# Attention with paired heads: all 64 rows of each half of the array filled in the score matmuls

## The reference

```
mod = (silu(c) @ wmod).reshape(8, 6, 1, 256)      # sa, ca, ga, sb, cb, gb; |gates| at least 0.25
h = layernorm(x) * (1 + ca) + sa
q, k, v = split(h @ w_in.T)                       # 16 heads of 16 columns
attn = softmax(causal(q @ k.T * 16 ** -0.5))      # 1024 x 1024 for each head
x = x + ga * ((attn @ v) @ w_out.T + b_out)
h = layernorm(x) * (1 + cb) + sb
r = sigmoid(mix(h, mu_r) @ W_r); kk = relu(mix(h, mu_k) @ W_k) ** 2
out = x + gb * (r * (kk @ W_v))                   # mix: a blend of each token with the one before it
```

## Time and the profile before

| what | value |
|---|---|
| time, median of 3 runs | 1929.98 us (1923.19 to 1935.57) |
| the profiled execution | 1931.11 us, span 1929.2 us |
| mean granted clock of TensorE | 0.798 |
| TensorE busy | 1640.5 us (85%) |
| VectorE busy | 1100.7 us (57%) |
| ScalarE busy | 924.7 us (48%) |
| GpSimd busy | 618.7 us (32%) |

### The profile page before, as it was taken

One profiled execution on the slowest core, in us unless ns is written; L12 is line 12 of the kernel. 1 busy time (PEld: TensorE's weight loads), 2 busy tenths in 40 slices (PEclk: granted clock), 3 DMA queues, 4 the chain that ended last, 5 costly groups with the idle time before them and its releaser, 6 DMA issues.

```text
span 1929.2 us, 34555 instructions
## 1 busy us (share of the span) xinstructions
PE 1640.5 (85%) x10856; PEld 929.0 (48%) x10856; DVE 1100.7 (57%) x2246; ACT 924.7 (48%) x1859; POOL 618.7 (32%) x750
## 2 busy tenths in 40 slices
PE   4698999898889989889898988889888998988854
PEld 2353445444554545454554545445454454544354
DVE  4656646756565655756566564666656555666232
ACT  2055545555455544545554553554544455545512
POOL 3012102433333332443323333333324432233455
PEclk7696859788986888778896787968897688978656
DMA  2311122111321122111221112211231112111100
GB/s 93 81 38 40 44 82 57 39 46 47 92 55 37 48 56 82 40 48 48 85 57 34 44 47 85 58 40 38 63 87 40 48 45 68 49 46 37 51 29 17
DMA packets 79864, 103.37 MB, mean 54 GB/s; under 512 B 22576, under 2 KB 43320, under 8 KB 79680
## 3 DMA queue, kind: packets, MB, share of 16 engines
q1 hardware_dynamic: 76544, 91.86, 17.4%
q0 software_dynamic: 2560, 8.39, 1.2%
q10 hardware_dynamic: 576, 0.79, 0.2%
HBM read 31.74 MB, written 8.94 MB: 21 GB/s over the span
## 4 chain that ended last, share of the span: by engine, by line
PE 63%; DVE 19%; issue 8%; ACT 5%; POOL 2%; SPq 1%; DMA 1%; DVEq 0%; ACTq 0%; POOLq 0%
PE val_ps L1120 14%; PE row_ps L1088 11%; PE col_ps L1051 10%; DVE max_a L874 9%; PE dense_ps L1130 8%; PE dense_ps L1132 6%; PE dense_ps L1131 6%; PE row_ps L1099 4%; PE dense_ps L1149 2%; DVE mixed L982 2%; DVE max_b L874 2%; ACT weights L715 1%; DVE gated L966 1%; DVE mix_out L990 1%; PE row_ps L1069 1%
## 5 line engine op out<-in xcount | busy, mean ns | idle before, releaser
L715 ACT ACTIVATE weights<-col_ps 128x512 f32<-128x512 f32 (+2 forms) x1280 | 635.3, 557 | 644.1 <-PE col_ps L1051 639.0
L874 DVE TENSOR_REDUCE max_a<-row_ps 128x1 f32<-128x512 f32 (+3 forms) x896 | 541.8, 644 | 402.2 <-PE row_ps L1099 251.4
L1088 PE MATMUL row_ps<-k_stack,q_stack 48*128 48x512 f32 (+3 forms) x1536 | 467.7, 469 | 108.8 <-DVE max_a L874 77.4
L1051 PE MATMUL col_ps<-q_stack,k_stack 50*128 50x512 f32 (+3 forms) x1536 | 425.8, 466 | 45.9 <-ACT weights L715 37.2
L604 POOL TENSOR_SCALAR_AFFINE_SELECT weights<-weights 128x512 f32<-128x512 f32 x256 | 169.0, 660 | 845.7 <-ACT weights L715 844.3
L1120 PE MATMUL val_ps<-weights,v_ones 128*32 128x512 f32 (+3 forms) x3072 | 405.0, 606 | 3.9 <-POOL weights L604 3.9
L1088 PEld LDWEIGHTS row_ps<-k_stack,q_stack 48*128 48x128 f32 x1536 | 228.0, 223 | 340.1 <-DVE max_a L874 186.4
L874 DVE TENSOR_REDUCE max_b<-row_ps 128x1 f32<-128x384 f32 (+3 forms) x384 | 215.1, 594 | 199.3 <-PE row_ps L1099 197.0
L1051 PEld LDWEIGHTS col_ps<-q_stack,k_stack 50*128 50x128 f32 x1536 | 212.8, 219 | 135.6 <-ACT weights L715 82.7
L1099 PE MATMUL row_ps<-mask_fill,mask_ident 64*128 64x64 bf16 (+1 forms) x2048 | 165.7, 233 | 0.0
L1120 PEld LDWEIGHTS val_ps<-weights,v_ones 128*32 128x32 f32 x3072 | 65.6, 118 | 88.8 <-issue 41.7
(11 more groups left out here) (122 smaller groups left out, 2173.3 us busy)
## 6 DMA issues: line engine op xcount, KB each, us to landing
q_stack<-q_part SPq DMA_DIRECT2D x384, 64.0 KB, 2.2
k_stack<-k_part SPq DMA_DIRECT2D x372, 64.0 KB, 2.2
xa<-in_x SPq DMA_DIRECT2D x8, 1024.0 KB, 5.6
att<-val_out SPq DMA_DIRECT2D x64, 128.0 KB
recips<-recip_rows SPq DMA_DIRECT2D x32, 256.0 KB
xq<-in_x SPq DMA_DIRECT2D x28, 256.0 KB, 3.7
out<-xq POOLq DMA_DIRECT2D x28, 256.0 KB, 2.8
q_stack<-max_rows SPq DMA_DIRECT2D x256, 4.0 KB
```

Source lines behind the costliest of these rows:

```text
L715: nc.scalar.activation(weights[:, t % 2, heads[0]:heads[-1] + 1:2, 0:q1 - q0], col_ps[bank][:, 0:n * (q1 - q0)].rearrange("p (h q) -> p h ...
L874: nc.vector.reduce_max(dest, bank[:, 0:len(heads) * (k1 - k0)].rearrange("p (h k) -> p h k", h=len(heads)), AX_X).then_inc(max_done, 1)
L1051: last = nc.tensor.matmul(col_ps[bank][:, i * (q1 - q0):(i + 1) * (q1 - q0)], stack_at(k_stack[s % 2], rows, heads[i], P * j, P * (j + 1)) ...
L1088: last = nc.tensor.matmul(banks[odd][:, n * width:(n + 1) * width], stack_at(q_stack[stack], rows, heads[n], P * i, P * (i + 1)), stack_at ...
```

## The change

The maximum's two rows move from rows 48 and 49 of each half to rows 62 and 63. The 14 rows between, 48 to 61, are now in the contraction: they are zero in `q_stack`, set once at the start by GpSimd, and 1.0 in `k_stack`, as they were before, so that they add nothing to a score. `row_pair` contracts 62 rows for each head in place of 48, `score_columns` 64 in place of 50.

```
--- before.py
+++ after.py
@@ -44,6 +44,7 @@
 ROWS = len(Q_PARTS) * HD
 MROWS = 2
 ROW_TILE = 64
+MAX_AT = ROW_TILE - MROWS
 FILL = 2 * 2 * len(Q_PARTS) * 16
 PLACED = 2 * MROWS * 16
 
@@ -463,7 +464,7 @@
 
                 for part in range(MROWS):
                     for odd in range(2):
-                        row, lo = ROW_TILE * odd + ROWS + part, 8 * (2 * part + odd)
+                        row, lo = ROW_TILE * odd + MAX_AT + part, 8 * (2 * part + odd)
                         sp.dma_start(stack[row:row + 1, half].rearrange("p g n -> p (g n)").bitcast(F32),
                                      max_rows[half][lo:lo + 8, :].bitcast(F32)).then_inc(max_placed[half], 16)
 
@@ -569,8 +570,10 @@
             nc.gpsimd.memset(ident[:], 0.0)
             nc.gpsimd.memset(mask_ident[:], 0.0)
             nc.gpsimd.memset(mask_fill[:], 0.0)
-            nc.gpsimd.memset(neg_half[:], -0.5).then_inc(consts_zero, 1)
-            pool.wait_ge(consts_zero, 1)
+            nc.gpsimd.memset(neg_half[:], -0.5)
+            for stack in q_stack:
+                nc.gpsimd.memset(stack[:].bitcast(F32), 0.0).then_inc(consts_zero, 1)
+            pool.wait_ge(consts_zero, 2)
             nc.gpsimd.affine_select(out=ident[:], in_=ident[:], compare_op=ALU.not_equal, fill=1.0, base=0,
                                     pattern=[[-1, P]], channel_multiplier=1).then_inc(consts_done, 1)
 
@@ -1047,7 +1050,7 @@
                         bank, ago = bank_of(COLS * s + c + odd, COLS * G)
                         if i == 0:
                             wait(pe, exp_done, exp_index(b, s, c + odd) + (1 - ago))
-                        rows = slice(ROW_TILE * odd, ROW_TILE * odd + ROWS + MROWS)
+                        rows = slice(ROW_TILE * odd, ROW_TILE * (odd + 1))
                         last = nc.tensor.matmul(col_ps[bank][:, i * (q1 - q0):(i + 1) * (q1 - q0)],
                                                 stack_at(k_stack[s % 2], rows, heads[i], P * j, P * (j + 1)),
                                                 stack_at(q_stack[s % 2], rows, heads[i], q0, q1),
@@ -1083,7 +1086,7 @@
                     for odd, heads in enumerate(pair):
                         if n == 0:
                             banks[odd] = row_bank(b, s, u + odd)
-                        rows = slice(ROW_TILE * odd, ROW_TILE * odd + ROWS)
+                        rows = slice(ROW_TILE * odd, ROW_TILE * odd + MAX_AT)
                         end = n == len(heads) - 1 and not diagonal
                         last = nc.tensor.matmul(banks[odd][:, n * width:(n + 1) * width],
                                                 stack_at(q_stack[stack], rows, heads[n], P * i, P * (i + 1)),
```

## The result

The changed kernel takes 1844.28 us (median of 4 runs, 1840.81 to 1848.19), against 1926.59 us for the kernel before on the same chip: a ratio of 0.9571, 95% interval 0.9523 to 0.9619, so 4.3% faster. The forecast was 2.3% (1886 us): the sign, and the clock as the way to it, were as forecast; the size was almost twice that. The profiled execution takes 1840.81 us, its span 1838.9, at a mean granted clock of 0.865 against 0.798.

A forecast was written before the change was run, and what follows sets the result against it. TensorE was taken as the bound, busy 85% at a mean clock of 0.798. All costs were 0; the clock gain of 44 us took 1931.1 to 1887, 1886 us at the median, range 1860 to 1912.

The forecast's parts named there:

- Three steps were taken at zero: Costs of more rows in score matmuls and weight loads, of the maximum's moved DMAs, and of two GpSimd memsets: each 0.
- the bound of zero: Weight loads of the score matmuls: extra rows cost between zero and 19 us in all; zero was taken.
- a cover that reached to 19 us: At the start, TensorE's first products end at 19.0 us, before it needs the constants, which the memsets delay to about 7.5.
- the forecast's case against the rule of the Trainium skill: Score stretches 5.00 of 5.00 us busy had clock 0.50, so busy share doesn't set it; the rule would leave 1930 us.
- The rival in which zero data doesn't count: Part of the no-change rival: the clock grant ignores rows whose data is zero; 1930 us, chance 0.32 for no change.
- Three of twelve are 15 us in a batch: Of twelve low-clock 5 us stretches in a batch, the three with at least 62% scores turn to full clock.
- the 5 us cut: The fifth batch, 950 to 1180 us, cut into 46 stretches of 5 us; twelve lie at clock 0.50 to 0.59.
- my three: The stretches at 1005, 1050 and 1070 us of the fifth batch, with 64, 62 and 73% scores, expected to turn.
- my 5.5 for the whole batch: Gain from three turned stretches at 1.8 us each, of a batch's 226 to 228 us; eight batches give 44 us.
- my rate: Time gained per clock gained, 0.73, the middle of 0.47 (second quarter) and one for one (last quarter of a batch).
- A larger gain: Rival: the full level holds on into the next stretches, six of twelve turn, 88 us gained, 1842 us; chance 0.08.
- The slower case: Rival: TensorE pauses for VectorE's maxima and clock drops move into dense and value work; up to 1967 us, chance 0.08.

The follow-up runs named there:

- first experiment: A separate kernel without the reference's work: 16 phases of back-to-back 512-column matmuls, varying rows and data; clock 1.00 with 128 and 96 rows, 0.50 with 80 and 64.
- sixth: The changed kernel with seven of the 14 query rows at 1.0 and seven at -1.0: ratio 0.9557 to the kernel before, median 1843.0 us.
- tenth: The changed kernel with rows 48 to 61 of the key stacks cleared too, so zeros in both operands: ratio 0.9624 to the kernel before, median 1848.6 us.
- thirteenth run: The changed kernel with only the stacks of the second and fourth quarter filled, the others keeping 50 and 48 rows: ratio 0.9745 to the kernel before, median 1868.3 us.
- runs 2: The changed kernel with the row maxima back at 48 rows, the score columns still contracting 64: ratio 0.9775 to the kernel before.
- 3: The changed kernel with the maximum's rows at 54 and 55, so 54 and 56 rows are contracted: ratio 0.9817 to the kernel before.
- 7: The changed kernel with row maxima at 62 rows but score columns at 48, without the maximum's two rows: ratio 0.9863 to the kernel before.

## Why the prediction was right in kind and too small

**Costs.** Three steps were taken at zero, and nothing speaks against it. More rows cost no time on matmuls or loads: in the groups after, the loads of 62 rows take 211 ns and those of 128 rows 216, so that nearly all of the 35 ns between them in the earlier trace rows was the clock's, and the bound of zero, which I took, was the right one. The maximum's moved rows and the memsets left no trace in the time; the memsets ended at 5.1 us, under a cover that reached to 19 us.

**The clock follows the filled rows.** This was the forecast's case against the rule of the Trainium skill (TensorE: Matmul & The Clock Gate, "What's actually happening"), by which busy-ness alone decides and the time would stay. The first experiment decides it: at 7.00 of 7.00 us busy, 80 rows get 0.50 and 96 rows 1.00. If "busy" in that rule is read as the profile's busy share, the rule fails here. The rival in which zero data doesn't count falls with the first, sixth and tenth runs.

**The step that failed: "Three of twelve are 15 us in a batch".** The mean clock tells the true number. Time at the lower level was (1 - 0.798) x 2 x 1929 = 779 us and is (1 - 0.865) x 2 x 1839 = 497 us: 282 us less, where three stretches a batch make 120. In the 5 us cut, 12 stretches have become 4. By quarter, the same sum with the fifth batch's rows gives 2, 24, 5 and 13 us less at the lower level, some 44 us, where the forecast has 15. I had judged each stretch by the share of scores in it, 62% or more, and left out the rest because "the rest of their work fills the array already". That is true of those matmuls, but the share of scores in a stretch doesn't tell whether it turns: the stretches at 1125 and 1160 (0.79 and 1.41 us of scores in 5.00) turned, and the one at 1050, with 3.00 of 4.84 us, stayed at 0.50 with its rows filled. So one of my three turned and one in part, and what turned was mostly what I had left out. The second quarter, around which my three lay, gave 5.6 us of this batch's 13.2; that this is close to my 5.5 for the whole batch is chance, since it comes from 24 us that turned and not from 15. The third and fourth quarters gave the other 7.5 us. The thirteenth run shows the fourth quarter's part apart; runs 2, 3 and 7 show that the gain grows with the rows and with the kinds of product that are filled. Why one stretch turns and another doesn't stays open, and whether TensorE falls to the lower level less often or comes back from it sooner was not separated by any run.

**What a point of clock is worth.** I took 0.73% of time for 1% of clock, the middle of 0.47 and 1. The two profiled executions give 4.7% of time for 8.4% of clock, 0.56. With the measured time that turned and my rate, the gain would have been 282 x 0.365 = 103 us, where 90 us were measured, 0.32 us for each that turned: this error was the smaller one, and it went the other way. The upper end of my rate was read too low besides: 52.90 against 49.20 us is 7.5% of time for 6.25% of clock, 1.2 for one and not one for one, and the middle would have been 0.83, further off.

**The rivals.** "A larger gain", with six stretches turned, 1842 us and a chance of 0.08, is what happened in size. That it fits almost to the microsecond is luck: 282 us are seven stretches a batch and not six, at a lower rate. It got too low a chance for the reason above; its argument, that the full level holds on into the next stretch, isn't shown. The slower case didn't come: VectorE's share of the chain did rise by three points and the waits for it by 2 us in the 512-column groups, but no quarter in the batch shown got longer.

## What to carry to other kernels

When TensorE is the bound and its granted clock is at the lower level in stretches where it is never idle, look at how much of the array the matmuls there name, rows above all: padding a short contraction with rows of zeros up to the half of the array cost no time per matmul here and lifted the clock from 0.798 to 0.865. Start its price from all the time at the lower level (779 us here, of which 282 turned) and give each microsecond that turns less than the half that it could return at most (0.32 here); don't pick stretches by which kind of work dominates in them. Extra matmuls put in only to keep the clock up cost more than they gave here.

## What the runs showed of the hardware that I had not expected

- The data had no part in it that these runs can tell: 128 rows of zeros hold 1.00 as random numbers do, and in the kernel 14 rows of zeros, of zeros against ones, or of +1 and -1 give the same time (1848.6 against 1849.1 us, and 1843.0 against 1841.5).
- A dense product of 128 rows by 128 columns, one after the other with a fresh weight load each, never leaves 0.50, though it shows as 8.00 of 8.00 us busy; float32 transposes of the same size, 67 of them begun in 7 us, run at 1.00.
- In the batches shown here a quarter of the same work tends to a few durations: the fourth one at 52.7 and 52.9 us (0.80 of the clock), at 49.1, 49.1, 49.2 and 50.1 us (0.85), or at 47.5 us (0.91).
